# Taking TensorE's filler matmuls of ones out of the attention steps of a fused attention and mixture-of-experts block

## Chip, cores and metric

One core of one Trainium2 chip. The metric is device microseconds of one execution, lower is better; a comparison is a median over several runs.

## What is computed

A MetaFormer block on x of (8, 192, 16, 16) float32: windowed attention with a relative position bias on channel-normalised x, added to x, then a top-1 mixture of nine experts on token-normalised x, added again.

```python
x = x + conv_ref(_ln_c(x), Wq, Wk, Wv, Wo_w, Wo_b, rel_pos_bias, rel_coords)
#   q, k, v = projections of 8x8 windows, 12 heads of 16
#   p = softmax(q k^T / 4 + bias);  o = p v;  out = Wo o + Wo_b
t = _to_tokens(x)
t = t + ffn_ref(_ln_t(t), Ws, bs, W1, b1, W2, b2)
#   route = argmax softmax(t Ws + bs);  h = gelu(t W1[e] + b1[e]);  out = h W2[e] + b2[e]
#   final = common, if route == 0, else p * sel + (1 - p) * common
```

## The kernel before

The 2048 tokens are 16 tiles of 128. Attention is float32. It runs as a software pipeline written out by hand: in step s each engine goes once through a fixed list of stages (PE_PROGRAM, ACT_PROGRAM, DVE_PROGRAM, POOL_PROGRAM), and a stage with lag n works on tile s - n. So one step of TensorE touches up to six tiles, and the list alone sets the order on an engine; semaphores hold the engines to each other. Where a stage depends on the stage before it in the same step, an engine waits inside the step; where it depends on the step before, there is slack.

TensorE's list for one step, with the line of each in the profile: x_to_tokens (L1011, transposes of x), project_values (L1047), weights_to_keys_1 (L1074, transposes of the second half of the softmax weights), output_projection (L1116), xh_to_channels (L65), project (L1032, queries and keys), scores (L1063), attend (L1099), ranks (L1134 to L1141, every fourth step only), logits (L1156), normed_to_channels (L1018), weights_to_keys_0 (L1074, the first half), keep_busy (L1089), attended_to_channels (L1108). The step ends with L1108, which waits for the normalised attention output `on` from VectorE (L888).

VectorE's list: statistics of x (L829, L831), the copy of values (L853), the copy of transposed weights (L876), the residual (L893 to L898), xh (L905), normed (L823), the key blocks (L841, after project), the bias onto the scores (L862, `sc`), the reciprocal and `on` (L884, L888, after attend), slots (L946 to L950, every fourth step), the logits' copy (L911), the row maximum (L869), choose (L934 to L939, every fourth step). GpSimd does the softmax shift (L533), part of each normalisation and part of the expert weights' split; ScalarE copies PSUM out and does the exponentials (L690).

keep_busy(t) has lag 1, so it runs in steps 1 to 16. It multiplies a matrix of ones by the identity into p_t[1], the PSUM tile that weights_to_keys_1 writes later; nothing reads what it leaves. From t = 3 on it first waits for pT_kept[1], VectorE's copy of an earlier use of that tile in the same step.

After the attention steps come the expert tiles: 128 tokens each, first layer L1530, second layer L1559, on the same PSUM tiles. Five of them lie among the last attention steps. From about 229 us on, they run alone, and the end is a gather of rows (L1279) and the output.

Of the kernel before, what the change touches and what calls it, by code (L numbers as in the profile page):

```python
# [78 lines left out]
def build(nc, x, Wq, Wk, Wv, Wo_w, Wo_b, rpb, rel, Ws, bs, W1, b1, W2, b2, out):  # L79
# [4 lines left out]
    with ExitStack() as whole:  # L84
# [43 lines left out]
        base16 = sbw("base16", [128, NE], F16)  # L128

        stage_1 = attention(nc, locals())  # L130
        stage_2 = experts(nc, locals(), stage_1)
        fused(nc, stage_1, stage_2, whole)
# [40 lines left out]
def attention(nc, g):  # L173
# [17 lines left out]
    with ExitStack() as ctx:  # L191
# [3 lines left out]
        def pb(name, cols, dt=F32):  # L195
            return g["whole"].enter_context(nc.psum_tensor(name, [128, cols], dt))

        def sem(name):
            return g["whole"].enter_context(nc.semaphore(name))
# [58 lines left out]
        p_t = [pb("p_t0", 512), pb("p_t1", 512)]  # L258
# [61 lines left out]
        pT_kept = [sem("pT_kept0"), sem("pT_kept1")]  # L320
# [26 lines left out]
        PE_PROGRAM = (("x_to_tokens", 0), ("project_values", 1), ("weights_to_keys_1", 4),  # L347
                      ("output_projection", 5), ("xh_to_channels", 7), ("project", 1), ("scores", 2),
                      ("attend", 4), ("ranks", 0), ("parked_outputs", DRAIN_STEP + 1), ("logits", 7), ("normed_to_channels", 0),
                      ("weights_to_keys_0", 3), ("keep_busy", 1), ("attended_to_channels", 4))  # L350
        ROUTING = ("choose", "ranks", "slots")
        LATE_E = NE - 1
        LATE_STEP = DRAIN_STEP + 1
# [23 lines left out]
        def stages(step, program, functions, split):  # L377

            by_name = {f.__name__: f for f in functions}
            quarter = 2 * (step - FIRST_SPLIT)  # L380
            for name, lag in program:
                if name == "split":
                    if 0 <= quarter < QUARTERS:
                        split(quarter // 4, (0, 2, 1, 3)[quarter % 4])
                        quarter += 1
                elif name in ROUTING:
                    group, rest = divmod(step - ROUTE_STEP + (name == "choose"), GROUP)
                    if rest == 0 and 0 <= group < NT // GROUP:
                        by_name[name](group)
                elif 0 <= step - lag < NT:  # L390
                    by_name[name](step - lag)
# [573 lines left out]
        def tensor_part(pe, hidden, outputs, counts):  # L965
            pe.wait_ge(consts, 1)

            def transpose_weights():

                pe.wait_ge(watt_loaded, 16 * 4)  # L970
                for m, bank in enumerate((p_qk, p_v, p_t[0], p_t[1])):
                    for k in range(2):
                        for r in range(2):
                            mm = pe.transpose(bank[0:CH, k * C + r * CH:k * C + (r + 1) * CH],
                                              watt[:, m, r, k * CH:(k + 1) * CH], ident[0:CH, 0:CH])
                    mm.then_inc(wt_mm, 1)
                pe.wait_ge(tab_loaded, 16 * 3)
                for k in range(2):
                    mm = pe.transpose(p_s[0:TH, k * NH:(k + 1) * NH], tab[:, k * TH:(k + 1) * TH],
                                      ident[0:NH, 0:NH])  # L980
                mm.then_inc(tab_mm, 1)
# [99 lines left out]
            def weights_to_keys_1(t):  # L1081
                weights_to_keys(t, 1)

            def keep_busy(t):

                if t >= 3:
                    pe.wait_ge(pT_kept[1], t - 2)
                for _ in range(3):
                    pe.matmul(p_t[1][:, :], ident16[:, :],  # L1089
                              ones16[:, :].unsqueeze(1).to_broadcast([128, 4, 128]), start=True, stop=True)  # L1090

            def attend(t):
                for h in range(2):
                    pe.wait_ge(pT_kept[h], t + 1)
                    pe.wait_ge(v_kept[h], t + 1)
                bank_read("attend", t, P_V_READ)
                for n, pair in enumerate(PAIRS):
                    for w in range(2):
                        mm = pe.matmul(p_v[w * L:(w + 1) * L, pair * 2 * VW:(pair + 1) * 2 * VW],  # L1099
                                       pT[:, t % 2, n, w * L:(w + 1) * L], v2[:, t % VB, w, pair, :, :],  # L1100
                                       start=True, stop=True)
                mm.then_inc(pv_mm, 1)
# [63 lines left out]
            for step in range(STEPS):  # L1166
                if step == 1:
                    transpose_weights()
                stages(step, PE_PROGRAM, (x_to_tokens, normed_to_channels, project, project_values, scores,
                                          weights_to_keys_0, weights_to_keys_1, attend, keep_busy, attended_to_channels,  # L1170
                                          output_projection, xh_to_channels, logits, ranks, parked_outputs), None)
                if 0 <= step - DRAIN_STEP < DRAIN:
                    hidden(step - DRAIN_STEP)

        return dict(sync=sync_part, gpsimd=gpsimd_part, scalar=scalar_part, vector=vector_part, tensor=tensor_part,
                    p_x=p_x, p_n=p_n, p_qk=p_qk, p_v=p_v, p_s=p_s, p_t=p_t, xhT_ready=xhT_ready, lg_kept=lg_kept,
                    w1_tail=w1_tail, w1_hi=w1_hi, w1_lo=w1_lo, w2_hi=w2_hi, w2_lo=w2_lo, b1_stored=b1_stored, ohc_ready=ohc_ready,
# [444 lines left out]
```

## Time and profile before

| | us |
|---|---|
| median of 3 runs | 335.38 |
| lowest, highest | 334.8, 336.01 |
| profiled execution | 336.16 |
| its span, first to last instruction | 334.4 |

The profiled execution is 0.8 us above the median, and 1.8 us of it lie outside the span. The page gives busy time of each engine, the span in 40 slices of 8.36 us with TensorE's granted clock in tenths of full speed, the chain of work that ended last, and the costliest groups. The clock has two levels here, 1.00 (2.4 GHz) and 0.50 (1.2 GHz). The profile has no record of the clock before 27.69 us and prints 1.00 there.

### The profile page before, as it was taken

The numbers are of one execution on the slowest core, as the hardware profiler recorded it, in microseconds if no ns is written. First come the engines' busy times: TensorE is split into PE (matmuls) and PEld (weight loads), VectorE is DVE, ScalarE is ACT, GpSimd is POOL, SyncE is SP. The second block draws the span as 40 slices with busy tenths as digits, with TensorE's granted clock in tenths as the row PEclk, the third lists the DMA queues.
The fourth block names the chain that finished last, engine by engine and source line by source line (L and its number), as shares of the span: only waits on it lengthen the run. The fifth ranks groups of instructions, "written<-read, shape, count | busy, mean of one in ns | idle before, by whom it ended". The sixth has DMA issues, their size and how long they took to land.

```text
span 334.4 us, 9567 instructions
## 1 busy us (share of the span) xinstructions
PE 277.8 (83%) x3525; PEld 240.9 (72%) x3525; DVE 245.7 (73%) x529; ACT 192.1 (57%) x418; POOL 158.5 (47%) x211
## 2 busy tenths in 40 slices
PE   0199479989999798889677898939999999999963
PEld 0185357767777676666477797939999999999951
DVE  1444689999999899999744368946898899884552
ACT  1535457777777477777464639504645455454632
POOL 4002287888887779898836658400000000001772
PEclk9999969999999799999678999978999999999995
DMA  7981254424243433333300011222223322310364
GB/s 267 220 184 25 50 161 129 121 84 120 85 119 84 121 99 110 101 100 112 103 27 17 18 54 65 97 83 50 70 73 76 78 74 68 73 40 25 94 166 119
DMA packets 39328, 31.44 MB, mean 94 GB/s; under 512 B 17271, under 2 KB 38202, under 8 KB 39027
## 3 DMA queue, kind: packets, MB, share of 16 engines
q1 hardware_dynamic: 37459, 25.07, 28.4%
q0 software_dynamic: 1536, 3.67, 3.5%
q10 hardware_dynamic: 288, 2.10, 1.6%
q8 instruction: 29, 0.48, 0.6%
q14 instruction: 16, 0.13, 0.1%
HBM read 18.70 MB, written 7.33 MB: 78 GB/s over the span
## 4 chain that ended last, share of the span: by engine, by line
PE 50%; DVE 11%; issue 9%; DMA 9%; POOL 8%; ACT 7%; SPq 3%; POOLq 0%; DVEq 0%; ACTq 0%
PE p_s L1530 8%; PE p_t L1530 7%; PE p_v L1559 6%; PE p_qk L1559 6%; PE p_qk L1032 6%; POOL w1d L1279 4%; DVE sc L862 4%; PE p_v L1047 3%; PE p_x L1116 3%; DMA sorted_tokens<-xhl,slot 2%; PE p_t L1074 2%; DVE kc L841 2%; DMA xhl<-n_L_conv_rel_coords_dram 2%; PE p_n L1108 1%; ACT q L675 1%
## 5 line engine op out<-in xcount | busy, mean ns | idle before, releaser
L1444 DVE TENSOR_TENSOR hp<-hf,hp 128x384 f16<-128x384 f32 x78 | 44.2, 574 | 28.5 <-ACT hf L1323 28.5
L1279 POOL DMA_INDIRECT w1d<-sorted_outputs,row x16 | 15.5, 972 | 99.6 <-DMA sorted_outputs<-yo 95.0
L1320 ACT ACTIVATE hp<-p_t 128x384 f16<-128x384 f32 x38 | 18.7, 492 | 35.8 <-PE p_t L1530 35.8
L1320 ACT ACTIVATE hp<-p_s 128x384 f16<-128x384 f32 x40 | 19.6, 491 | 27.5 <-PE p_s L1530 27.5
L539 POOL TENSOR_SCALAR rstd<-mv 128x1 f32<-128x1 f32 x32 | 7.1, 222 | 47.6 <-DVE mv L831 41.3
L1530 PE MATMUL p_t<-tokT,w1d 128*128 128x128 f16 (+1 forms) x360 | 23.9, 227 | 5.6 <-DMA tokT<-sorted_tokens 5.6
L1032 PE MATMUL p_qk<-xnT,wT 96*128 96x128 f32 x192 | 26.8, 293 | 0.0
L1530 PEld LDWEIGHTS p_t<-tokT,w1d 128*128 128x128 f16 (+1 forms) x360 | 22.6, 102 | 5.8 <-issue 5.8
L1032 PEld LDWEIGHTS p_qk<-xnT,wT 96*128 96x128 f32 x192 | 24.7, 205 | 0.5 <-issue 0.2
L533 POOL TENSOR_TENSOR sc<-sc,mx 128x768 f32<-128x768 f32 x16 | 23.5, 1468 | 0.1
L1431 DVE COPY w1d<-w1s 128x3072 f16 x23 | 21.9, 954 | 0.6 <-issue 0.6
L574 POOL TENSOR_TENSOR w2s<-w2stage,w2s 128x576 f16<-128x576 f32 x16 | 20.4, 1277 | 2.2 <-ACT w2s L735 1.8
L1074 PE MATMUL p_t<-ident,sc 128*128 128x128 f32 x96 | 17.8, 298 | 3.3 <-ACT sc L690 3.3
L1530 PE MATMUL p_s<-tokT,w1d 128*128 128x128 f16 (+1 forms) x330 | 20.5, 219 | 0.0
L1559 PE MATMUL p_v<-w2d,hp 128*128 128x192 f16 x216 | 19.8, 246 | 0.0
L605 POOL DMA_INDIRECT sorted_tokens<-xhl,slot x16 | 17.0, 1061 | 5.8 <-issue 2.9
L690 ACT ACTIVATE sc<-sc 128x768 f32<-128x768 f32 x16 | 13.5, 844 | 10.6 <-POOL sc L533 10.5
L1323 ACT ACTIVATE hf<-p_s 128x384 f32<-128x384 f32 x40 | 19.4, 486 | 0.0
L1530 PEld LDWEIGHTS p_s<-tokT,w1d 128*128 128x128 f16 (+1 forms) x330 | 19.4, 97 | 0.0
L541 POOL TENSOR_TENSOR rstd<-rstd,minus_half 128x1 f32<-128x1 f32 x32 | 18.1, 567 | 2.7
L1323 ACT ACTIVATE hf<-p_t 128x384 f32<-128x384 f32 x38 | 18.5, 488 | 0.0
L1018 PE MATMUL p_n<-ident,xn 128*96 128x128 f32 x32 | 7.1, 308 | 13.3 <-DVE xn L823 13.3
(212 smaller groups left out, 773.6 us busy)
## 6 DMA issues: line engine op xcount, KB each, us to landing
w2stage<-in_L_ffn_W_dram SPq DMA_DIRECT2D x18, 288.0 KB, 3.3
w1stage<-in_L_ffn_W_dram SPq DMA_DIRECT2D x18, 192.0 KB
w1stage<-in_L_ffn_W_dram SPq DMA_DIRECT2D x36, 96.0 KB
sorted_outputs<-yo SPq DMA_DIRECT2D x23, 96.0 KB, 1.6
xin<-in_x_dram SPq DMA_DIRECT2D x8, 192.0 KB, 4.3
out_dram<-outc SPq DMA_DIRECT2D x8, 192.0 KB, 2.3
sorted_tokens<-void SPq DMA_DIRECT2D x9, 128.0 KB, 1.7
xhl<-n_L_conv_rel_coords_dram ACTq DMA_DIRECT2D x1, 1024.0 KB, 6.2
```

What stands on the lines that cost most here:

```text
L533: pool.tensor_tensor(s, s, mx[:, t % 2, :].unsqueeze(2).to_broadcast([128, NH, L]), ALU.subtract).then_inc(s_sub, 1)
L541: pool.tensor_tensor(r, r, minus_half[:, :], ALU.pow).then_inc(done, 1)
L574: pool.tensor_tensor(w2s[:, e, 1, r, :], w2stage[:, r, :], w2s[:, e, 0, r, :], ALU.subtract).then_inc(w2_lo, 1)
L1032: mm = pe.matmul(p_qk[:, c * T:(c + 1) * T], wT[:, k, c * 128:(c + 1) * 128], xnT[:, t % 2, k, :], start=(k == 0), stop=(k == 1))
L1074: mm = pe.transpose(p_t[h][:, n * T:(n + 1) * T], sc[:, t % SB, pair * 2 * L:(pair + 1) * 2 * L], ident[:, :])
L1279: pool.indirect_dma_start(out=sel[:, t % GB, :], out_offset=None, in_=ys, in_offset=bass.IndirectOffsetOnAxis(ap=row[:, t:t + 1], axis=0)) ...
L1320: act.activation(hp[:, n % 2, 0, HF * h:HF * h + HF, :], p_h[n % 2][h][:, 0:HF * T].rearrange("p (f t) -> p f t", f=HF), ACT.Gelu, scale=1 ...
L1323: act.activation(hf[:, n % 2, h, :], p_h[n % 2][h][:, 0:HF * T], ACT.Gelu, scale=1.0 / SF).then_inc(h_act[h], 1)
L1431: dve.tensor_copy(w1d[:, j % 2, :, :], w1s[:, e, :, :]).then_inc(w1_copied, 1)
L1444: dve.tensor_tensor(hp[:, n % 2, 1, HF * h:HF * h + HF, :], hf[:, n % 2, h, :].rearrange("p (f t) -> p f t", f=HF), hp[:, n % 2, 0, HF * h ...
L1530: mm = pe.matmul(p_h[n % 2][f // HF][:, (f % HF) * T:(f % HF + 1) * T], w[0:rows, a, f * 128:(f + 1) * 128], xT[0:rows, b, :], start=(m == ...
L1559: mm = pe.matmul(y, hp[:, n % 2, a, f, :], w[:, b, f, :], start=False, stop=(f == NF - 1 and m == 2))
```

## The change

keep_busy is taken out of TensorE's list and its function is deleted. That removes 16 groups of three matmuls of 128x512 float16, three weight loads each, and from the fourth group on the wait ahead of them. Nothing else is edited: the constants `ones16` and `ident16` stay, since other stages use them.

```diff
-                      ("weights_to_keys_0", 3), ("keep_busy", 1), ("attended_to_channels", 4))
+                      ("weights_to_keys_0", 3), ("attended_to_channels", 4))
-            def keep_busy(t):
-
-                if t >= 3:
-                    pe.wait_ge(pT_kept[1], t - 2)
-                for _ in range(3):
-                    pe.matmul(p_t[1][:, :], ident16[:, :],
-                              ones16[:, :].unsqueeze(1).to_broadcast([128, 4, 128]), start=True, stop=True)
```

The order of everything else stays as it was, on all engines. On TensorE, one steady step around the end of its list, before (`p_n<-ident,on` is attended_to_channels, `p_v<-v,pT` is attend, `sc` the softmax weights):

```order
L1099 MATMUL p_v<-v,pT 64x34 x12
L1156 MATMUL p_x<-ws,xhT 128x9 x5
L1018 MATMUL p_n<-ident,xn 96x8x2x8 x2
L1074 MATMUL p_t<-ident,sc 128x128 x3
L1089 MATMUL p_t<-ones,ident 128x512 x3
L1108 MATMUL p_n<-ident,on 96x2x8x8 x2
L1011 MATMUL p_x<-ident,xin 128x96 x2
```

and the same place in the changed kernel, whose lines behind the deleted function are numbered 8 lower:

```order
L1091 MATMUL p_v<-v,pT 64x34 x12
L1148 MATMUL p_x<-ws,xhT 128x9 x5
L1018 MATMUL p_n<-ident,xn 96x8x2x8 x2
L1074 MATMUL p_t<-ident,sc 128x128 x3
L1100 MATMUL p_n<-ident,on 96x2x8x8 x2
L1011 MATMUL p_x<-ident,xin 128x96 x2
```

The transposes of L1074 now stand directly ahead of the stage that waits for VectorE.

## Rows read from the trace of the kernel before

**Rows 1.** The page: busy time of each engine; tenths of busy in 40 slices, granted clock.

```profile
PE 277.8 (83%) x3525; PEld 240.9 (72%) x3525; DVE 245.7 (73%) x529; ACT 192.1 (57%) x418; POOL 158.5 (47%) x211
...
PEclk9999969999999799999678999978999999999995
```

**Rows 2.** Steady attention steps: length, busy (instructions) of PE, PEld, DVE, ACT, POOL, clock, DMA.

```profile
52.00:155.00 103.00, 92.31 (x1117) 71.83 (x1114) 96.75 (x207) 76.66 (x166) 84.67 (x111) 0.98 0.36 104
```

**Rows 3.** Chain of waits at full clock, behind L1108 to the bias: start us, us.

```profile
102.56 0.81 PE p_v L1047 x16
103.37 0.48 PE p_t L1074 x3
103.85 0.65 PE p_x L1116 x4
...
104.73 1.41 PE p_qk L1032 x12
...
109.35 0.96 DVE sc L862
```

**Rows 4.** Waits of TensorE from 52 to 156 us: total us, times, longest.

```profile
PE p_n L1108 <- DVE on L888: 10.3, 13, 1.4
```

**Rows 5.** The fillers' line: durations in ns (min/median/max), first and last start us.

```profile
L1089 PE MATMUL p_t<-ones,ident x48: 379/379/634, 27.9 to 153.9; 128*128 128x512 f16 x48
```

**Rows 6.** Timeline of TensorE, one steady step: start us, us, idle before in brackets.

```profile
100.15 0.49 PE L1074 MATMUL p_t<-ident,sc 128*128 128x128 f32 x3
100.48 0.81 PE L1089 MATMUL p_t<-ones,ident 128*128 128x512 f16 x3
101.97 0.42 PE L1108 MATMUL p_n<-ident,on 128*96 128x128 f32 x2 [0.68 <-DVE on L888]
```

**Rows 7.** Chain of waits, the position bias from memory.

```profile
32.73 3.66 DMA bias<-bias_by_head
```

**Rows 8.** Chain of waits, the first step after the low stretch of 41 us.

```profile
45.82 1.28 PE p_t L1089 x3
```

**Rows 9.** Stretches: length, PE busy (instructions), granted clock, DMA share, GB/s.

```profile
48.17:113.02 64.85, 58.57 (x722) 1.00 0.39 109
113.02:116.44 3.42, 3.42 (x17) 0.50 0.57 167
...
160.81:171.05 10.24, 7.28 (x63) 0.50 0.31 96
```

**Rows 10.** Chain of waits through the low stretch and to the next bias.

```profile
112.91 0.70 PE p_t L1074 x3
113.61 1.28 PE p_x L1116 x4
...
115.32 2.00 PE p_qk L1032 x12
...
119.24 0.96 DVE sc L862
```

**Rows 11.** Chain of waits, the biases of two later steps.

```profile
128.38 0.96 DVE sc L862
...
136.75 0.96 DVE sc L862
```

**Rows 12.** Timeline of TensorE near the start, all at half clock.

```profile
21.15 2.93 PE L1032 MATMUL p_qk<-xnT,wT 96*128 96x128 f32 x12
```

**Rows 13.** Timeline of TensorE, the step in which the clock fell.

```profile
108.72 0.81 PE L1089 MATMUL p_t<-ones,ident 128*128 128x512 f16 x3
110.90 0.42 PE L1108 MATMUL p_n<-ident,on 128*96 128x128 f32 x2 [1.36 <-DVE on L888]
```

**Rows 14.** Timeline of TensorE, a similar step in which the clock held.

```profile
127.69 0.81 PE L1089 MATMUL p_t<-ones,ident 128*128 128x512 f16 x3
129.92 0.42 PE L1108 MATMUL p_n<-ident,on 128*96 128x128 f32 x2 [1.42 <-DVE on L888]
```

More of the change, by code:

```diff
@@ L1169, in tensor_part @@
                 stages(step, PE_PROGRAM, (x_to_tokens, normed_to_channels, project, project_values, scores,
-                                          weights_to_keys_0, weights_to_keys_1, attend, keep_busy, attended_to_channels,
+                                          weights_to_keys_0, weights_to_keys_1, attend, attended_to_channels,
                                           output_projection, xh_to_channels, logits, ranks, parked_outputs), None)
```

## The prediction

> **What bounds the kernel now.** I start from the page. TensorE is busy 83% of the span and VectorE 73%, and the clock line is 9 nearly everywhere, with a 6 or 7 in a few slices [rows 1]. The change lies in the attention steps alone, so the average over the span says little; from 52 to 155 us VectorE is busy 96.75 of 103 us and TensorE 92.31 of 103, at a mean clock of 0.98 [rows 2]. Neither has much room, and the chain of waits shows why: in each step it goes from `on` (VectorE) to L1108 on TensorE, along TensorE without a break through L1011, L1047, L1074, L1116, L65 to the end of project (L1032), and from there over VectorE's key blocks and the bias `sc` back to `on` [rows 3]. So a step is a ring with two halves. TensorE's half, from the start of L1108 at 101.97 [rows 6] to the end of L1032 at 104.73 + 1.41 = 106.14, is 4.17 us of a step of about 8 us. In the other half TensorE does scores, attend, logits and three groups of transposes, and then waits for `on`: 13 waits in 13 steps, 10.3 us in all, the longest 1.4 [rows 4]. That is the only wait of any size that it has there.
>
> **What the change removes.** The fillers are 48 matmuls, the first at 27.9 and the last at 153.9 us, 379 ns each at full clock [rows 5]; three of them overlap to 0.81 us [rows 6]. In the 13 steps from 52 to 155 us each group stands directly ahead of the wait at L1108, and that wait is above zero every time. With the group gone TensorE only comes to the same wait sooner: 13 x 0.81 = 10.5 us of matmul time go, and the wait grows from 10.3 to up to 20.8 us. On the path this is worth nothing. The wait for pT_kept ahead of the group goes too; the trace shows no idle time for it, so also nothing. VectorE, ScalarE, GpSimd and the DMAs lose and gain no instruction, and no data pass through the fillers.
>
> Three groups lie outside these steps. Those at 27.9 and 32.7 us stand ahead of a wait for the position bias, whose DMA is in the chain until 36.4 us [rows 7], so they are worth nothing. The one at 45.82 us is in the chain, 1.28 us at half clock [rows 8]. This is the single place where the change gives time back at once. Its ends: 1.28 us if all behind it moves forward, 0 if VectorE's work hides it. But the work that moves forward was done at full clock from 48.17 us on [rows 9] and now falls partly before that time, when the clock is still low, at about twice the price. I take half: **-0.6 us**.
>
> **What the change moves: the clock.** The dense half of a step is at the mercy of TensorE's clock, since it is in the chain. The price of a low stretch can be read off one that happened. The clock fell at 113.02 and came back at 116.44 [rows 9], in the dense half of a step. In that step L1116 took 1.28 us in the chain against 0.65, L1074 0.70 against 0.48, and L1032 2.00 against 1.41, part of it low [rows 3, 10]; that is 1.4 us more on these three. From bias to bias this step took 119.24 - 109.35 = 9.89 us; the next step of the same kind (both hold slots) took 136.75 - 128.38 = 8.37 us [rows 3, 10, 11]. So a fall costs 9.89 - 8.37 = **1.5 us**, all of that and a little of the stages between; VectorE hides next to nothing of it. If the whole dense half were low, the price would be up to double its length: L1032 then takes 2.93 us [rows 12] against 1.41, which for 4.17 us makes about +3.7.
>
> How often will it fall? Before, it fell in one of the 13 steps. Ahead of that fall TensorE ended a filler group at 109.53, stood idle 1.36 us, and did only two short groups of transposes before 112 us [rows 13]. A very similar gap, 127.69 + 0.81 = 128.50 to 129.92 us, 1.42 us idle, had no fall [rows 14]. The low stretch at 160.81 comes 7 us after the last filler [rows 5, 9]. So before, the clock was on the edge where a gap reached 1.4 us, and ordinary steps, with 0.68 us idle behind 0.81 us of full-width 512-column matmuls [rows 6], were safe. After the change an ordinary step has idle from the end of L1074 at 100.64 to L1108 at 101.97, 1.33 us, as much as the one that fell, and what stands ahead of it is transposes and small matmuls where it was fillers; the long gaps grow from 1.4 to about 2.2 us. All 13 steps then look like the two doubtful ones or worse. At the odds of those two (one of two) 6.5 of 13 would fall, and at worst all 13. I take 8, a little above half because the longer gaps are worse than either, hence 7 new ones: 7 x 1.5 = **+10.5 us**.
>
> The Trainium skill has a rule that speaks against this change: the page TensorE: Matmul & The Clock Gate, section A second HAM failure mode: psum-queue depth-cycling, says that short idles between groups of matmuls can already make the clock swing between its two levels, and that the loss is in the returning to half speed and back. The fall at 113.02 agrees.
>
> **The sum**, against the profiled execution: 336.16 - 0.6 + 10.5 = 346.1 us. That execution is 0.8 us above the median of the runs; against 335.38 it gives **345.3 us**, which I predict. Behind 155 us I put nothing: the stretch at 160.81 to 171.05 is low already, and its place may move by a few us either way, which is worth about one fall, 1.5 us, of either sign.
>
> **Rivals.**
> *No new falls.* The fillers do nothing for the clock, and TensorE's own work holds it. For it: a gap of 1.42 us passed without a fall [rows 14]. Against it: none of the low stretches of [rows 9] begins right behind a filler. Then only the term at 45.82 us is left, 335.38 - 0.6 = 334.8 us; with the whole 1.28 it would be 334.1, which is the faster side, and if in addition the one fall at 113 vanished because the gaps move, 332.6. It decides at the point where 1.33 to 2.2 us idle still hold the clock. This is the rival that ends on the other side. The same page's closing table, in the section Why this matters for your kernels, puts the danger only in longer idle gaps between bursts than any of these; by that rule this rival would be right. The fall behind 1.36 us idle does not bear it out, so its chance stays small.
>
> *A fall in every step.* Every gap is now beyond the edge: 12 new falls x 1.5 = +18, 353 us. If the clock then also stays low for more than one step's dense half, as it did for 10.24 us from 160.81 [rows 9], each of 13 steps pays up to 3.7 us, +48, 383 us. For it: the gaps are all alike. Against the second form: on 113.02 the clock came back after 3.42 us, with TensorE busy all the time, and the dense half is there in each step.
>
> *Falls, but hidden.* VectorE's own 96.75 us of 103 [rows 2] leave 0.5 us a step, so it could be the real bound, and a late TensorE would matter less. At a third of the price, 7 x 0.5 = 3.5, this gives 338.3 us. The 9.89 against 8.37 us speaks against it.
>
> **Chances.** Around the forecast (5 to 10 new falls, 342 to 350 us): 0.52. A fall in nearly every step, 351 to 357: 0.16; mostly half clock, beyond 357: 0.06. Few or hidden falls, 336.4 to 342: 0.10. No new falls, within 1 us of 335.38: 0.10; faster than that, 0.06. The range of **335.6 to 357 us** leaves out the half clock (0.06), the faster case (0.06) and most of the one with no new falls (0.07). A measurement of this kernel tells about 0.3% (1 us) from no change: faster 0.06, same 0.10, slower 0.84.
>
> **What would show it.** In the changed kernel's profile: the clock line has 6 to 8 in many of the slices between 50 and 155 us, and the mean clock there is about 0.88 (8 stretches of 3.4 us at half in some 113 us); steps with a low stretch take about 9.6 us from bias to bias and others about 8.1; the wait at L1108 has grown to some 1.5 us a step. From 229 us on the two timelines are the same but for the shift. The prediction is wrong if the clock line keeps its 9s with the fillers gone, if it falls and steps do not get longer, or if it stays low over whole steps.

## The result and the profile after

The changed kernel takes 344.87 us (median, 341.24 to 346.11), beside 335.69 us for the kernel before. The ratio is 1.0225, with a 95% interval of 1.0161 to 1.0289: slower, by 9.2 us between the medians, where 9.9 were forecast. Medians here are over all runs of a kernel, while each ratio is taken over those within 1.5% of the fastest of their kernel, so it is not the quotient of the medians (here 1.0273, inside the interval). The profiled execution took 344.38 us with a span of 341.8, against 336.16 and 334.4.

The page of the changed kernel, its first lines:

```profile
span 341.8 us, 9471 instructions
...
PE 275.7 (81%) x3477; PEld 245.2 (72%) x3477; DVE 244.0 (71%) x529; ACT 192.0 (56%) x418; POOL 158.5 (46%) x211
...
PEclk9999769989699698798989899996999999999995
```

TensorE has 48 matmuls fewer and only 2.1 us less busy time, since others got longer; VectorE's work is the same 529 instructions. The clock line answers to the one in [rows 1]: in the slices of the attention steps, the 9s are broken by 6, 7 and 8.

The stretches with the low clock, by length, PE busy (instructions), granted clock, DMA share, GB/s. Ahead of them the steady steps as a whole, which answer to [rows 2], and as the last row the longest one at full clock, which holds the expert tiles that run alone:

```profile
52.00:155.00 103.00, 86.68 (x993) 0.88 0.33 95
68.97:72.39 3.42, 3.42 (x28) 0.50 0.33 97
86.04:92.87 6.83, 6.83 (x43) 0.50 0.21 58
113.35:120.17 6.82, 6.03 (x36) 0.50 0.46 136
133.83:140.66 6.83, 6.83 (x41) 0.50 0.31 96
154.31:157.72 3.41, 3.41 (x26) 0.50 0.52 171
236.23:331.80 95.57, 93.66 (x1375) 1.00 0.28 73
```

The mean clock from 52 to 155 us is 0.88 against 0.98. There are five low stretches, 27.3 us together, where before there was one of 3.42 [rows 9]. In the low stretches TensorE was busy all the time or nearly so, and each begins within 0.8 us of the start of attended_to_channels, before or behind it, so they lie on the dense half of the step. The fifth begins at 154.31 us and lies almost wholly behind the window of 52 to 155 us. The stretch of the expert tiles at full clock is 95.57 us long in both kernels, with 93.66 us of it busy here and 93.54 before, so nothing was lost there.

The wait of TensorE ahead of attended_to_channels (now L1100), 52 to 165 us, answers to [rows 4]:

```profile
PE p_n L1100 <- DVE on L888: 17.4, 13, 2.1
```

It grew from 10.3 to 17.4 us, that is, 7.1 of the 10.5 us of removed matmuls turned into waiting.

One step without and one with a fall, in the changed kernel's chain of waits (start us, us). The first two rows enclose an ordinary step, the rest lie in the step from 84.19 to 95.02:

```profile
75.87 0.96 DVE sc L862
84.19 0.96 DVE sc L862
...
86.47 1.48 PE p_v L1047 x16
87.95 0.83 PE p_t L1074 x3
88.78 1.28 PE p_x L1108 x4
90.06 0.43 PE p_n L65 x4
90.48 2.60 PE p_qk L1032 x12
...
95.02 0.96 DVE sc L862
```

(L1108 here is output_projection, L1116 before.) Step against step, bias to bias: 84.19 - 75.87 = 8.32 us with the clock high, 95.02 - 84.19 = 10.83 us with nearly the whole dense half at half clock. The excess over the 8.11 us that the same step took before (84.13 to 92.24) is 2.7 us; the rows show it against [rows 3]: 0.67 on L1047, 0.35 on L1074, 0.63 on the projection, 1.19 on L1032, 2.8 together. Timeline of TensorE, what it did just ahead of that fall at 86.04:

```profile
83.92 0.49 PE L1074 MATMUL p_t<-ident,sc 128*128 128x128 f32 x3
85.73 0.42 PE L1100 MATMUL p_n<-ident,on 128*96 128x128 f32 x2 [1.33 <-DVE on L888]
```

This is the 1.33 us of idle behind transposes that the prediction expected from an ordinary step. The same wait two steps later had no fall; the clock stayed at full speed until 113.35 us:

```profile
105.03 0.42 PE L1100 MATMUL p_n<-ident,on 128*96 128x128 f32 x2 [1.32 <-DVE on L888]
```

The five steps with a fall, bias to bias, beside the same steps of the kernel before. For the third, where the kernel before had its own fall, the two steps of the run with five fillers stand in its place, which had none (8.73 and 8.65 us):

| clock falls, us | low, us | wait at L1100, us | step, us | without a fall | more | more in the next step |
|---|---|---|---|---|---|---|
| 68.97 | 3.42 | 1.73 | 9.24 | 8.12 | 1.1 | 0.2 |
| 86.04 | 6.83 | 1.33 | 10.83 | 8.11 | 2.7 | 0.3 |
| 113.35 | 6.82 | 2.01 | 10.74 | 8.73 | 2.0 | 0.5 |
| 133.83 | 6.83 | 2.07 | 10.81 | 8.37 | 2.4 | 0.0 |
| 154.31 | 3.41 | 1.78 | 9.07 | 7.47 | 1.6 | 0.0 |

Together that is 9.9 us in the steps themselves and 1.0 in the next ones, 10.9 us for five falls, or 2.2 us each. The other eight waits had no fall: seven of 0.96 to 1.06 us and the one of 1.32 us.

### The profile page after: what moved, and what is told of

It is laid out like the page before. It is cut to its first block, busy times and chain, and to the rows that moved or that the text cites. A ratio compares the mean times of both kernels' runs of the same rounds, so it can differ in the third digit from the quotient of the medians.

```text
span 341.8 us, 9471 instructions
## 1 busy us (share of the span) xinstructions
PE 275.7 (81%) x3477; PEld 245.2 (72%) x3477; DVE 244.0 (71%) x529; ACT 192.0 (56%) x418; POOL 158.5 (46%) x211
## 4 chain that ended last, share of the span: by engine, by line
PE 51%; DVE 11%; issue 10%; POOL 9%; DMA 8%; ACT 7%; SPq 3%; POOLq 0%; DVEq 0%; ACTq 0%
PE p_s L1522 7%; PE p_t L1522 7%; PE p_qk L1032 7%; PE p_v L1551 6%; PE p_qk L1551 6%; PE p_v L1047 4%; POOL w1d L1271 4%; DVE sc L862 4%; PE p_x L1108 4%; PE p_t L1074 2%; DVE kc L841 2%; DMA xhl<-n_L_conv_rel_coords_dram 2%; DMA sorted_tokens<-xhl,slot 1%; PE p_n L1100 1%; POOL sc L533 1%
## 5 line engine op out<-in xcount | busy, mean ns | idle before, releaser
L1032 PE MATMUL p_qk<-xnT,wT 96*128 96x128 f32 x192 | 29.7, 314 | 0.0
L1032 PEld LDWEIGHTS p_qk<-xnT,wT 96*128 96x128 f32 x192 | 27.8, 227 | 0.5 <-issue 0.2
L1074 PE MATMUL p_t<-ident,sc 128*128 128x128 f32 x96 | 19.5, 319 | 3.9 <-ACT sc L690 3.9
L1100 PE MATMUL p_n<-ident,on 128*96 128x128 f32 x32 | 7.3, 315 | 17.7 <-DVE on L888 17.7
L1108 PE MATMUL p_x<-woT,oT 97*128 97x192 f32 (+1 forms) x64 | 17.3, 403 | 3.6 <-ACT oT L703 3.4
L1047 PE MATMUL p_v<-wT,xnT 96*64 96x96 f32 x256 | 18.3, 300 | 2.1 <-ACT xnT L668 2.1
```

Of the source, the lines that this page charges most:

```text
L1032: mm = pe.matmul(p_qk[:, c * T:(c + 1) * T], wT[:, k, c * 128:(c + 1) * 128], xnT[:, t % 2, k, :], start=(k == 0), stop=(k == 1))
L1047: mm = pe.matmul(p_v[h * L:(h + 1) * L, w * CH:(w + 1) * CH], xnT[:, t % 2, k, w * L:(w + 1) * L], by_parity[:, k, h, :, :], start=(k == 0 ...
L1074: mm = pe.transpose(p_t[h][:, n * T:(n + 1) * T], sc[:, t % SB, pair * 2 * L:(pair + 1) * 2 * L], ident[:, :])
L1108: mm = pe.matmul(p_x[:, 0:C], oT[0:CH + 1 - k, k, :], woT[0:CH + 1 - k, k, :], start=(k == 0), stop=(k == 1))
```

## Experiments

All are the kernel before with one edit. In their series the kernel before was itself spread, 335.6 to 341.4 us, so ratios carry wide intervals, and much rests on the profiles, of which there is one for each kernel.

**The wait alone.** The matmuls of keep_busy go, its wait stays.

```diff
                 if t >= 3:
                     pe.wait_ge(pT_kept[1], t - 2)
-                for _ in range(3):
-                    pe.matmul(p_t[1][:, :], ident16[:, :], ...)
```

> keep_busy keeps its place and its wait for pT_kept[1], but issues no matmul. Clock theory (the matmuls hold TensorE's clock, the wait does nothing): as the changed kernel, 341 to 347 us, mean granted clock from 52 to 155 us about 0.88, 5 or so low stretches. Rival (the wait or the place in TensorE's queue did the work, by what it lets start when): as before, 335 to 337 us, one low stretch there.

Measured: 346.47 us, ratio 1.0242 (1.0171 to 1.0313), six low stretches between 52 and 162 us. The first three:

```profile
72.43:75.85 3.42, 3.42 (x18) 0.50 0.28 86
89.50:92.91 3.41, 3.41 (x23) 0.50 0.31 87
106.57:113.39 6.82, 6.82 (x42) 0.50 0.22 59
```

So it behaves as the changed kernel. The wait did nothing; what counted is the matmuls. The length of the one wait ahead does not settle a fall, though: the fourth low stretch begins at 120.22 us, 2.7 us behind the end of a wait of 1.04 us (117.49), the length that passed seven times in the changed kernel.

**One filler in place of three.**

```diff
-                for _ in range(3):
+                for _ in range(1):
```

> One filler matmul a step in place of three. Clock theory: a third of the cover, so fewer low stretches than the 5 of the changed kernel but more than 1; 2 to 4 of them at 1.1 to 2.7 us each give 338 to 343 us. Rival (any matmul in the gap will do, since it is the length of the idle that counts and one matmul splits or shortens it): as before, 335 to 337. Rival (one is no better than none): 341 to 347.

Measured: 344.14 us, ratio 1.0166 (1.0052 to 1.0281). Three low stretches from 52 to 155 us, one of them long:

```profile
69.33:72.74 3.41, 3.41 (x27) 0.50 0.35 92
113.70:117.11 3.41, 3.41 (x18) 0.50 0.49 150
130.76:144.42 13.66, 13.66 (x105) 0.50 0.31 90
```

Three falls lie between one and five, but the time is above the 338 to 343 us expected, since the third stretch held over more than a step. One filler is a little cover, not enough: its interval doesn't separate it from none. This kernel also showed the longest low times of all. In its profile a fourth stretch lasts 20.48 us (164.90 to 185.38). And one of its four runs took 445.39 us at a mean clock of 0.575, where the other three took 340.11 to 344.87; that run left no profile, so what TensorE did in it is not known.

**Fillers only from t = 3 on.**

```diff
+                if t < 3:
+                    return
-                if t >= 3:
-                    pe.wait_ge(pT_kept[1], t - 2)
+                pe.wait_ge(pT_kept[1], t - 2)
```

> Fillers only from t = 3 on; the groups near 28, 33 and 46 us are gone. The prediction's term for them was -0.6 us (range -1.28 to 0): 334.4 to 335.7. The comparison of the two traces says that from the first bias (L862) to the second steady one the changed kernel took 16.39 us and the kernel before 16.02, so by that the three groups are worth 0 or a little: 335.5 to 336.5. One low stretch from 52 to 155 us either way.

Measured: 338.84 us median, beside 337.64 for the kernel before, and not the 335.5 to 336.5 expected. Three of its four runs lie at 338.82 to 339.03 and one at 333.67, so the time is inconclusive. The profile is not: the low stretch near 41 us lasts 10.24 us here, and lasted 6.83 in the kernel before.

```profile
40.54:50.78 10.24, 6.53 (x38) 0.50 0.55 159
112.22:119.05 6.83, 6.83 (x41) 0.50 0.32 90
```

There is one low stretch near 113 us, as expected, but it is twice as long as before, and its step takes 11.43 us (109.81 to 121.24) against 9.89. That is time lost far behind the first three groups, and it blurs the comparison of the times further.

The longer stretch near 41 us comes back in every profile of this study whose start is otherwise as before: without the full group at 46 us (the changed kernel, the wait alone, one of three, this one, every other step) the stretch lasts 10.24 us, with it (before, behind the wait, five a step) 6.83. So the group costs 1.28 us in the chain [rows 8], and with it the clock comes back sooner. From the first bias to the third it took 52.43 - 36.41 = 16.02 us in the kernel before, 51.17 - 34.78 = 16.39 in the changed one and 52.93 - 36.07 = 16.86 here; the five profiles without the full group lie between 16.38 and 16.95.

**The same fillers behind the wait.**

```diff
-                      ("weights_to_keys_0", 3), ("keep_busy", 1), ("attended_to_channels", 4))
+                      ("weights_to_keys_0", 3), ("attended_to_channels", 4), ("keep_busy", 1))
```

> The same three fillers a step, but behind L1108 in TensorE's list and not ahead of its wait. Theory: the clock is held as before (0 to 2 low stretches from 52 to 155 us), but the group now lies in the half of the step that is in the chain, about 0.65 us a step (three at 216 ns start to start), 13 x 0.65 = +8.4: 342 to 345 us. Rival (TensorE has slack in every step wherever it is put, so place doesn't matter): 335 to 337.

Measured: 346.94 us, ratio 1.0314 (1.0236 to 1.0391), more than expected. Its chain of waits over one step at full clock:

```profile
88.01 0.96 DVE sc L862
89.55 0.42 PE p_n L1108 x2
89.97 0.65 PE p_t L1089 x3
90.62 0.17 PE p_x L1011 x2
...
96.77 0.96 DVE sc L862
```

The fillers are now in the chain with 0.65 us, and the step is 96.77 - 88.01 = 8.76 us where it was 8.12. That is the price expected. The clock was held less well, though: four low stretches from 52 to 155 us, 17.1 us in all and a mean clock of 0.92, against one of 3.42 before and 24.6 us in the changed kernel. An ordinary wait at L1108 is as long here as with no fillers, 1.33 us at 89.55. So place matters: within the wait a filler is free, and it also shortens the idle time there. Whether the weaker hold comes from the longer idle time or from the longer step, this run can't tell.

**Five in place of three.**

```diff
-                for _ in range(3):
+                for _ in range(5):
```

> Five fillers a step in place of three, same place. The group grows by 0.43 us, which the ordinary wait of 0.68 us ahead of L1108 still hides. Theory (matmuls ahead of the wait hold the clock, and cost nothing within it): the wait at L1108 falls from 10.3 to about 5 us, and the low stretch near 113 us goes or is rarer: 0 to -1.5 us against before. Rival (three already do all that can be done, and two more lie on the path): +0.43 x 13 = +5.6 us.

Measured: 336.09 us, ratio 0.9933 (0.9886 to 0.9979). The low stretch near 113 us is gone, and the wait has shrunk. Its longest stretch at full clock:

```profile
47.25:159.89 112.64, 105.33 (x1262) 1.00 0.37 108
```

The waits of TensorE from 52 to 156 us:

```profile
PE p_n L1108 <- DVE on L888: 5.6, 11, 0.9
```

In the steady steps the two more cost nothing, because the wait covers them: bias to bias is 8.12 us here too. The early group is not within a wait, and there they were paid for, 2.03 us in the chain against 1.28 [rows 8]:

```profile
45.46 2.03 PE p_t L1089 x5
```

From the first bias to the third it took 16.63 us, against 16.02. The chain of waits of this kernel also gives the length of the step from 109 us, the one in which the clock fell before, without a fall, and of the step behind it:

```profile
109.56 0.96 DVE sc L862
118.29 0.96 DVE sc L862
126.94 0.96 DVE sc L862
```

That is 8.73 us against 9.89 in the kernel before, and 8.65 against 9.14 in the next step [rows 3, 10, 11]. The 9.14 us (or 9.13) come back in every profile with a fall in the first of the two steps and none in the second, seven in all, and in neither profile without a fall, this one and the last of this study. So a fall also lengthens the step behind its own, by 0.5 us there.

**Every other step.**

```diff
-                for _ in range(3):
+                for _ in range(3 if t % 2 else 0):
```

> Three fillers in every other step only. Theory: about half of the changed kernel's extra low stretches, and only behind steps without fillers: 2 to 3 falls more than before, at 1.1 to 2.7 us each, +3 to +6 us against before, mean clock from 52 to 155 us 0.92 to 0.94. Rival (what counts is the mean load of TensorE over long stretches, not each gap): either nothing or all of the changed kernel's +9.

Measured: 345.38 us, ratio 1.0199 (1.0087 to 1.0311); as much as the full change, so the half that was expected of it was wrong. Its timeline shows the waits ahead of L1108 in steps without fillers, and below them stand the low stretches:

```profile
62.35 0.39 PE L1108 MATMUL p_n<-ident,on 128*96 128x128 f32 x2 [1.01 <-DVE on L888]
78.60 0.39 PE L1108 MATMUL p_n<-ident,on 128*96 128x128 f32 x2 [1.38 <-DVE on L888]
100.22 0.40 PE L1108 MATMUL p_n<-ident,on 128*96 128x128 f32 x2 [1.31 <-DVE on L888]
117.31 0.63 PE L1108 MATMUL p_n<-ident,on 128*96 128x128 f32 x2 [2.06 <-DVE on L888]
137.21 0.63 PE L1108 MATMUL p_n<-ident,on 128*96 128x128 f32 x2 [2.12 <-DVE on L888]
```

```profile
79.15:92.80 13.65, 13.65 (x97) 0.50 0.33 95
116.69:123.52 6.83, 6.03 (x36) 0.50 0.44 134
137.17:144.00 6.83, 6.79 (x40) 0.50 0.31 95
```

These three falls, at 79.15, 116.69 and 137.17, and a fourth at 157.66 behind a wait of 1.83 us, come in the wait of a bare step or within 0.7 us of its end; none follows a step with fillers. Two bare steps with waits of 1.01 and 1.31 us passed without one (62 and 100 us). So the places of the falls fit gaps that count one by one, but the time came out as the rival of the mean load had it, all and not half: the four stretches are low for 30.7 us together, more than the 27.3 us of the changed kernel, and the one from 79.15 us lasts over the next step too and eats what the fillers there would save.

**Fillers ahead of the first wait.** 19 more, ahead of the wait of 7.68 us for the first normed tile; fill(n) issues n of the same matmuls.

```diff
             def normed_to_channels(t):
+                fill({0: 19}.get(t, 0))
                 pe.wait_ge(xn_ready, t + 1)
```

> As before, with 19 more fillers ahead of the first wait for normed x (L1018, idle 7.68 us before 15.53). Theory (the clock is low at the start only because TensorE has done nothing yet, and its work to 27.66 us is in the chain): the clock is at 1.00 before 15.5 us, L1032's first group takes 1.4 and not 2.86 us, L1047's 0.8 and not 1.48, the position bias (L993) about 2 and not 3.56; the first bias onto the scores comes 3 to 5 us sooner, and the whole is 3 to 5 us shorter. Rival (other waits, of weights and tables, set the start): 0 to -1 us.

Measured: 334.76 us, the median of five runs from 330.93 to 339.19, beside 337.91 (335.71 to 341.39) for the kernel before; ratio 0.9803 (0.9671 to 0.9935). The interval is clear of no change, but the ranges overlap and the size of the gain is open. From the chain of waits:

```profile
18.17 0.88 PE p_v L1054 x16
19.05 1.53 PE p_qk L1039 x12
20.59 1.87 PE p_s L993 x32
...
32.23 0.97 DVE sc L862
```

Project's first group (L1039 here) takes 1.53 us and not 2.86, the position bias L993 1.87 and not 3.56, and the first bias onto the scores starts at 32.23 and not 36.41: 4.2 us sooner. The profile then gives 2 us back, since the next low stretch lasts 13.66 us and not 6.83:

```profile
35.70:49.36 13.66, 9.29 (x51) 0.50 0.46 128
```

**Fillers fitted to all the waits.** As above, and 24 ahead of the wait that ends at 44 us, none in the first three groups of keep_busy, five in ordinary steps, eight in the three steps whose wait was over 1.2 us, and three more groups behind.

```diff
             def normed_to_channels(t):
+                fill({0: 19, 3: 24}.get(t, 0))
...
             def keep_busy(t):
...
-                for _ in range(3):
-                    pe.matmul(p_t[1][:, :], ident16[:, :], ...)
+                fill({0: 0, 1: 0, 2: 0, 10: 8, 12: 8, 14: 8}.get(t, 5))
...
-                elif 0 <= step - lag < NT:
+                elif 0 <= step - lag < NT + 3 * (name == "keep_busy"):
```

> Fillers fitted to the waits: 19 at the start as in the run with the warm start, 24 ahead of the wait of 5.66 us that ends at 44.26, none in the first three groups, five in ordinary steps, eight in the three steps with a wait of 1.2 us or more, and three more groups behind the last attention step. Theory: the gains add up, -3 to -5 at the start, -1.5 to -2 around 41 to 50 us, -1.5 for the fall near 113: 327 to 331 us where before gives 335.5. Rival: the later parts give nothing, and it equals the warm start alone.

Measured: 331.38 us (330.6 to 332.06), ratio 0.9803 (0.9700 to 0.9906): faster than both kernels, and its four runs lie closer together than the twelve of the kernel before in the same series. Its stretches:

```profile
13.29:33.77 20.48, 15.35 (x173) 1.00 0.65 138
33.77:37.18 3.41, 3.41 (x18) 0.50 0.05 8
37.18:163.48 126.30, 116.63 (x1345) 1.00 0.38 110
```

The clock holds at 1.00 for 126 us, from before the second bias (41.55) to behind the last (151.73). The time is just above the range expected, 331.4 against 327 to 331, but the kernel before was at 337.9 here and not 335.5. The rival, that it equals the warm start alone, is refuted by the profiles and not by the times: from the first bias to the last it took 119.43 us here and 124.41 with the warm start, against 122.51 before, while the ratio of 0.9803 is the same as there and the ranges of the runs overlap.

## Why the prediction was right, point by point

- *The fillers lie in a wait and taking them away saves nothing there.* Right. The wait grew from 10.3 to 17.4 us, and in the steps without a fall bias to bias is as before (8.11 us from 58.52 to 66.63, against 8.12 from 59.78 to 67.90). Five a step cost nothing in these steps either, and behind the wait each three cost 0.65 us.
- *They hold the clock.* Right, and shown: with the wait kept and the matmuls gone there are six low stretches, where the changed kernel has five, and with five matmuls a step there is none. What it is in them that holds the clock, the shorter idle time or the work they give TensorE, is not separated by these runs; only their number and place were varied.
- *The count of falls.* 8 forecast, 5 in the profile. All 13 waits were taken to reach 1.33 us or more, and that premise was wrong: in the kernel before, four of them were only 0.3 to 0.4 us long (0.32 at 61.33, 0.41 at 121.00), and in the changed kernel seven came out at 0.96 to 1.06 us, and none of these had a fall. Of the six longer ones five had one. The odds of one in two were read from two gaps that were not as alike as they looked: behind the one that fell, TensorE stood idle once more, for 0.42 us, and behind the one that held it did not.

```profile
111.74 0.36 PE L1011 MATMUL p_x<-ident,xin 96*128 96x96 f32 x2 [0.42 <-DVE lg L911]
```

- *The length of the low stretches.* Three of the five lasted 6.8 us where all were taken at 3.4; why some last longer stays open. In sum 27.3 us were low, against 8 x 3.4 = 27.2 forecast, and the mean clock of 0.88 came out as said. That is luck: too many falls and too short ones cancel.
- *The price of a fall.* 1.5 us forecast. The comparison was not like with like: the step from 109.35 holds slots (L946 at 110.76), the one from 128.38 doesn't, contrary to what the prediction said. Against the same step without a fall (8.73 us, five fillers) it is 9.89 - 8.73 = 1.16 us, and with the 9.14 - 8.65 = 0.49 us of the step behind it 1.65, near the forecast by a working that did not hold. The falls of the changed kernel cost 1.3 and 1.6 us where the clock was low for 3.4 us, and 2.5 to 3.0 where it was low for 6.8, each with the step behind it. So 7 new falls at 1.5 us made +10.5, and five falls at 2.2, less the 1.65 of the one that was there before, made 9.2.
- *The first three groups, -0.6 us.* Wrong in sign: +0.4 us by the two traces (16.39 against 16.02), and up to +0.9 in the others without the full group, because with the group at 46 us the low stretch near 41 us is 3.4 us shorter. The prediction had seen that the work moves into the low stretch, and not that the stretch would grow.
- *The sum.* From the first bias on, the last one (158.92 before, 166.90 after) has lost (166.90 - 34.78) - (158.92 - 36.41) = 9.6 us: 9.2 by the falls and 0.4 in the first steps. The changed kernel's profile started with a gain of 36.41 - 34.78 = 1.6 us that is no effect of the change: the clock rose at 24.60 us, ahead of the place where the first filler had been, and at 27.69 in the profile before, so part of the position bias ran fast. With this gain counted in, the last bias is 8.0 us later and the span 7.4 us longer; the 0.6 us won back behind the last bias lie within the 1.5 us of either sign that the prediction allowed there. The 9.9 forecast stands against 9.6 without it. How close the two are is in part luck, since more falls were forecast, each at a lower price.
- *The rivals.* No new falls: refuted by the five. A fall in every step: no, 5 of 13, and in none of the four runs of the changed kernel the long form of 383 us. (Its term of 3.7 us a step is also too low by its own rows: 2.93 against 1.41 us on 4.17 us makes 4.5.) The long form is not out of reach, though: 13.66 us low did occur with one filler and with fillers in every other step, and one run with one filler took 445.39 us at a mean clock of 0.575. Hidden falls: refuted, since the step with the fall at 86.04 is longer by 2.7 us and its rows in the chain by 2.8. The rule of the Trainium skill on short idles between groups (TensorE: Matmul & The Clock Gate, A second HAM failure mode: psum-queue depth-cycling) agrees with the traces; the closing table of the same page of the Trainium skill (Why this matters for your kernels) advises against longer gaps than these only, and that is not enough for this kernel, where the clock fell behind 1.33 us of idle between transposes.

## What to carry to other kernels

Matmuls that compute nothing are not waste if they stand in a wait of TensorE and TensorE's dense part lies in the chain: look at what the granted clock does behind that wait before taking them out. Fit their number to the wait (free up to its length, paid for where there is no wait or behind it). Try some where TensorE idles before its first work in the chain: here the first bias came 4.2 us sooner, of which about 2 were given back. Half measures were not worth half: one filler a step, or three in every other step, could not be told from none. A saving of busy time on an engine that then waits is no saving.

## What the runs showed that was not expected

- The time of one kernel varies with where the clock falls. Of twelve runs of the kernel before, with the mean clock in brackets: 335.71 us (0.949), 336.18 (0.940), 340.22 (0.926), 340.46 (0.920). It is not the whole of it: 338.84 us came at 0.940 and 336.99 at 0.929. The kernel with fitted fillers spread over 1.5 us in four runs, at 0.954 to 0.965.
- The start, before any filler, was subject to the same: 1.6 us between the profiles of the two kernels, in which the clock rose at 24.60 and 27.69 us, and 4.2 us when it had been raised during the idle time ahead.
- Fillers in half of the steps were worth nothing measurable, 1.0199 against 1.0225: the low stretches began behind bare steps, and one of 13.65 us ran over the covered step behind it.
